# A linear-attention state in 32x32 tiles, output projections one head step earlier, and one row fetch moved ahead, in a fused attention and feed-forward kernel

## The reference

```python
# attn: 16 heads of 32 features; q, k, v, u = split(xn @ W_qkvu.T), q and k through silu
def step(kv, (qi, ki, vi)):                       # kv is [16, 32, 32]
    inter = (qi * q_decay) @ kv
    intra = ((qi @ ki.T) * diag_decay) @ vi
    kv = block_decay * kv + (ki * k_decay).T @ vi
    return kv, inter + intra
o = rms_normed(outs); attn = (u * o) @ W_out.T
# ffn: a router takes 256 of the 2048 rows; on them rms norm, q/k/v (16 heads of 128, 8 kv heads),
# rotary embedding, causal attention, wo, rms norm, silu(h @ w_gate) * (h @ w_up) @ w_down,
# gated with the router's sigmoid and put back at their places
```

## Time and profile before

| | |
|---|---|
| median of 3 runs | 508.22 us (507.51 to 508.35) |
| the profiled execution | 508.65 us |
| its span, first to last instruction | 506.9 us |
| granted clock of PE, mean | 0.990 |
| busy: PE, DVE, ACT, POOL | 486.5, 305.4, 231.6, 214.4 us |

### The profile page before, as it was taken

The page is one execution under the profiler, slowest core; times in us unless marked ns, Lnnn a source line. Parts: engine busy times, 40 slices in busy tenths (PEclk is TensorE's granted clock), DMA queues, the critical chain, the costliest instruction groups (busy, mean ns, idle before and its releaser), DMA issues.

```text
span 506.9 us, 10501 instructions
## 1 busy us (share of the span) xinstructions
PE 486.5 (96%) x4143; PEld 445.5 (88%) x4143; DVE 305.4 (60%) x615; ACT 231.6 (46%) x404; POOL 214.4 (42%) x191
## 2 busy tenths in 40 slices
PE   6998999999999999999999989799999999999994
PEld 6998899899998998999989888698888878999993
DVE  5879657764379888672555687997665535231221
ACT  7921132212255766512234226564667774545420
POOL 4002254232113311324268597434444413688872
PEclk8999999999999999999999999899999999999998
DMA  7924234113300110003525345354567462355503
GB/s 242 373 93 133 75 127 121 44 47 105 126 22 22 46 43 22 22 22 88 182 87 205 89 165 187 126 184 128 178 197 269 151 204 83 103 191 186 166 1 41
DMA packets 32880, 62.05 MB, mean 122 GB/s; under 512 B 3440, under 2 KB 3456, under 8 KB 32704
## 3 DMA queue, kind: packets, MB, share of 16 engines
q1 hardware_dynamic: 32288, 60.08, 36.0%
q0 software_dynamic: 544, 1.31, 1.4%
HBM read 48.27 MB, written 13.12 MB: 121 GB/s over the span
## 4 chain that ended last, share of the span: by engine, by line
PE 81%; DVE 8%; issue 3%; ACT 1%; POOL 0%; DVEq 0%; POOLq 0%
PE bank L1213 23%; PE bank L1167 10%; PE bank L1169 10%; PE bank L1168 10%; PE bank L1204 8%; PE bank L1276 3%; PE bank L1266 3%; PE bank L1232 3%; PE bank L1260 3%; DVE rope L862 3%; PE bank L1422 2%; PE bank L1443 1%; DVE rope L859 1%; DVE A L782 1%; PE bank L1183 1%
## 5 line engine op out<-in xcount | busy, mean ns | idle before, releaser
L1106 POOL TENSOR_TENSOR wlo<-raw,whi 128x512 fp32r<-128x512 f32 x96 | 125.5, 1341 | 86.7 <-ACT whi L516 86.7
L1091 POOL TENSOR_TENSOR state<-kv_new,state_dec 128x512 f32<-128x512 f32 x15 | 22.3, 1487 | 116.8 <-DVE kv_new L793 116.8
L1167 PE MATMUL bank<-HTh,whi 128*128 128x256 f32 x224 | 65.0, 290 | 3.0 <-DVE rope L862 3.0
L1169 PE MATMUL bank<-HTh,wlo 128*128 128x256 f32 x224 | 63.4, 283 | 0.0
L1168 PE MATMUL bank<-HTl,whi 128*128 128x256 f32 x224 | 63.3, 283 | 0.0
L782 DVE TENSOR_TENSOR A<-bank,DEC 128x512 f32<-128x512 f32 x64 | 39.7, 681 | 30.2 <-PE bank L1232 29.9
L516 ACT ACTIVATE whi<-raw 128x2048 fp32r<-128x2048 f32 x24 | 45.8, 1907 | 11.9 <-PE bank L1169 11.9
L1167 PEld LDWEIGHTS bank<-HTh,whi 128*128 128x128 f32 x224 | 42.9, 191 | 4.3 <-issue 3.8
L1168 PEld LDWEIGHTS bank<-HTl,whi 128*128 128x128 f32 x224 | 42.9, 192 | 0.3
L1169 PEld LDWEIGHTS bank<-HTh,wlo 128*128 128x128 f32 x224 | 42.9, 192 | 0.0
L1213 PE MATMUL bank<-xTh,WKh 128*128 128x256 f32 x128 | 37.5, 293 | 0.0
(11 more groups left out here) (237 smaller groups left out, 1361.3 us busy)
## 6 DMA issues: line engine op xcount, KB each, us to landing
X<-in_x SPq DMA_DIRECT2D x16, 256.0 KB, 4.5
xn_all<-XN SPq DMA_DIRECT2D x16, 256.0 KB, 2.7
uo_all<-uo SPq DMA_DIRECT2D x16, 256.0 KB, 2.4
raw<-in_wq SPq DMA_DIRECT2D x4, 1024.0 KB, 5.6
UR<-uo_all SPq DMA_DIRECT2D x16, 256.0 KB, 3.4
XR<-in_x SPq DMA_DIRECT2D x16, 256.0 KB, 3.1
raw<-in_wo SPq DMA_DIRECT2D x4, 1024.0 KB, 5.6
out<-XR SPq DMA_DIRECT2D x16, 256.0 KB, 2.1
```

Source lines behind the costliest of these rows:

```text
L1091: Q.tensor_tensor(state[:], kv_new[:], state_dec[:], ALU.add).then_inc(state_ok, 1)
L1106: ins = Q.tensor_tensor(low[:, k, :], raw[b % 3][:, k, :], high[:, k, :].bitcast(f32), ALU.subtract)
L1167: T.matmul(dst, lh, rh, start=first, stop=False)
L1169: return T.matmul(dst, ll, rh, start=False, stop=last)
```

## The change

The state, its decayed copy and the addition shrink to the 16 blocks of 32x32 (`[128, 4, 32]`). The carried-state product becomes 16 matmuls of 32 rows, 32 output rows and 128 columns, tile (r, r) for head 4j + r, all into `out_bank`; the new keys and values become 16 matmuls of 128 rows, 32 output rows and 32 columns. The mask and POOL's addition go; DVE adds straight from the bank. Output projections stand in steps 1 to 7 and 9 to 14, with the splits, the row fetches, the stores and the second fetches of x moved with them. SP fetches tile 4's rows ahead of the input and the stores of slot -1. PE turns tile 2 behind position 2.

```diff
-        qdec, sq, state, state_dec, kv_new = (at(n, kb, [P, NK, P]) for n, kb in (
-            ("qdec", 178), ("sq", 180), ("state", 184), ("state_dec", 186), ("kv_new", 188)))
+        qdec, sq = (at(n, kb, [P, NK, P]) for n, kb in (("qdec", 178), ("sq", 180)))
+        state, state_dec = (at(n, kb, [P, NK, DH]) for n, kb in (("state", 184), ("state_dec", 186)))
...
-        PT_AT, PV_AT, WO_AT, OUT_AT = 2, 3, 4, 2
+        PT_AT, PV_AT, WO_AT = 2, 3, 4
+        out_steps = [1, 2, 3, 4, 5, 6, 7, 9, 10, 11, 12, 13, 14]
+        out_at = {h: n for n, h in enumerate(out_steps)}
...
-            bank_jobs += [("out", h - OUT_AT)] if 0 <= h - OUT_AT < late_outs[0] else []
+            bank_jobs += [("out", out_at[h])] if h in out_at else []
...
             for N in slots_of_chunks:
+                if N == -1:
+                    load_xn(N + XT_AHEAD + 1)
                 for M in ln_tiles(N):
                     if M + 2 < N_TILES:
                         load_x(M + 2)
                     store_xn(M)
-                if NXN <= N + XT_AHEAD + 1 < N_TILES:
+                if NXN < N + XT_AHEAD + 1 < N_TILES:
                     load_xn(N + XT_AHEAD + 1)
...
             for h in range(STEPS):
-                if 2 <= h + 1 < N_TILES:
-                    load_uo(h + 1)
-                if 0 <= h - OUT_AT < late_outs[0]:
-                    store(h - OUT_AT)
-                if 2 <= h < N_TILES:
-                    load_x_again(h)
+                if h in out_at:
+                    n = out_at[h]
+                    load_uo(n + 2)
+                    store(n)
+                    load_x_again(n + 2)
+                    if h == out_steps[-1]:
+                        load_uo(n + 3), load_x_again(n + 3)
...
-                if 0 <= n + 1 < late_outs[2]:
-                    split_uo(n + 1)
+                if h == 0:
+                    split_uo(0)
+                if h in out_at:
+                    split_uo(out_at[h] + 1)
+                if h == out_steps[-1] + 1:
+                    split_uo(late_outs[1])
...
-            def state_part(N):
-
-                dve.wait_ge(kv_ps, N + 1), dve.wait_ge(state_ok, N)
-                V.tensor_tensor(kv_new[:], tiles4(turn_bank[:]), BM[:].unsqueeze(1).to_broadcast([P, NK, P]), ALU.mult)\
-                    .then_inc(kv_masked, 1)
+            def new_state(N):
+
+                dve.wait_ge(kv_ps, N + 1), dve.wait_ge(state_dk, N + 1)
+                V.tensor_tensor(state[:], turn_bank[:, 0:P].rearrange("p (k e) -> p k e", k=NK), state_dec[:], ALU.add)\
+                    .then_inc(state_ok, 1)
...
-                Q.tensor_tensor(state_dec[:], state[:], bdec.unsqueeze(2).to_broadcast([P, NK, P]), ALU.mult)\
+                Q.tensor_tensor(state_dec[:], state[:], bdec.unsqueeze(2).to_broadcast([P, NK, DH]), ALU.mult)\
                     .then_inc(state_dk, 1)
-
-            def new_state(N):
-
-                pool.wait_ge(kv_masked, N + 1), pool.wait_ge(state_dk, N + 1)
-                Q.tensor_tensor(state[:], kv_new[:], state_dec[:], ALU.add).then_inc(state_ok, 1)
...
-                for j in range(NK):
-                    ins = T.matmul(out_bank[:, j * P:(j + 1) * P], state[:, j, :], qdec[:, j, :], start=j == 0,
+                for h in range(NH):
+                    j, r = h // 4, h % 4
+                    rows = slice(DH * r, DH * r + DH)
+                    ins = T.matmul(out_bank[rows, j * P:(j + 1) * P], state[rows, j, :], qdec[rows, j, :], start=j == 0,
                                    stop=False, skip_group_check=True)
...
-                for j in range(NK):
-                    cols = slice(j * P, (j + 1) * P)
-                    ins = T.matmul(turn_bank[:, cols], kdec[:, cols], VT[N // CH % 2][:, N % CH, cols], start=True,
-                                   stop=True)
+                for h in range(NH):
+                    j, r = h // 4, h % 4
+                    cols = slice(DH * h, DH * h + DH)
+                    ins = T.matmul(turn_bank[DH * r:DH * r + DH, j * DH:(j + 1) * DH], kdec[:, cols],
+                                   VT[N // CH % 2][:, N % CH, cols], start=True, stop=True)
...
                 if N < 0:
                     in_position(N, 0)
                     in_position(N, 1)
-                    transposed(N + XT_AHEAD)
+                    if N == -1:
+                        transposed(N + XT_AHEAD)
                     in_position(N, 2)
+                    if N == -2:
+                        transposed(N + XT_AHEAD)
                     in_position(N, 3)
```

More of the change, by code:

```diff
@@ L270, in build @@
         q_dec, kt_ps, k_dec = sems("q_dec kt_ps k_dec")
-        s_ps, masked, inter_ps, kv_ps, kv_masked, pv_ps = sems("s_ps masked inter_ps kv_ps kv_masked pv_ps")
+        s_ps, masked, inter_ps, kv_ps, pv_ps = sems("s_ps masked inter_ps kv_ps pv_ps")
         state_dk, state_ok, uo_ok, sq_ok, sum_sq, rms_ps, ms_ok, r_ok = sems(
@@ L277, in build @@
         rank_ok, cnt_ps, oh_ok, idx_ps, idx_ok, pick_read = sems("rank_ok cnt_ps oh_ok idx_ps idx_ok pick_read")
-        dve_chain, pool_chain = sems("dve_chain pool_chain")
+        dve_chain, pool_chain, state_zero = sems("dve_chain pool_chain state_zero")
         fw_hi, fw_lo = sems("fw_hi fw_lo")
@@ L616, in _ @@
             for h in range(STEPS):
[L617 to L619 removed]
+                p, g = h - PT_AT, h - PV_AT
+                if h == 0:
[4 more added lines that the diff above has]
+                    split_uo(late_outs[1])
                 if h < FH:
@@ L636, in _ @@
                     normalised(h)
-                if 0 <= n < late_outs[0]:
-                    base(n)
+                if h in out_at:
+                    base(out_at[h])
                 if h in hi_after:
@@ L953, in _ @@
                 if 0 <= N < N_TILES - 1:
-                    state_part(N)
+                    new_state(N)
                 if N >= N_TILES - CH:
@@ L963, in _ @@
             for h in range(STEPS):
-                g, n = h - PV_AT, h - OUT_AT
+                g = h - PV_AT
                 if h < FH:
@@ L973, in _ @@
                     ins.then_inc(sm_ok, 1)
-                if 0 <= n + 1 < late_outs[2]:
-                    uo_low(n + 1)
+                if h == 0:
+                    uo_low(0)
+                if h in out_at:
+                    uo_low(out_at[h] + 1)
+                if h == out_steps[-1] + 1:
+                    uo_low(late_outs[1])
                 if h < FH:
@@ L982, in _ @@
                     stage(unit_of_step[h])
-                if 0 <= n < late_outs[0]:
-                    final(n)
+                if h in out_at:
+                    final(out_at[h])
                 if 0 <= g < FH:
@@ L1109, in _ @@
             ln_rstd(range(CH))
-            Q.memset(state[:], 0.0)
-            Q.memset(BM[:], 1.0).then_inc(pool_chain, 1)
-            blocks = BM[:].rearrange("p (r m) -> p r m", r=4)
-            pool.wait_ge(pool_chain, 5)
-            Q.affine_select(out=blocks, in_=blocks, compare_op=ALU.is_ge, fill=0.0, base=0, pattern=[[-DH, 4], [0, DH]],
-                            channel_multiplier=1).then_inc(pool_chain, 1)
-            pool.wait_ge(pool_chain, 6)
-            Q.affine_select(out=blocks, in_=blocks, compare_op=ALU.is_ge, fill=0.0, base=DH - 1,
-                            pattern=[[DH, 4], [0, DH]], channel_multiplier=-1).then_inc(bm_ok, 1)
+            Q.memset(state[:], 0.0).then_inc(state_zero, 1)
             ln_rstd(range(CH, NXN))
@@ L1249, in keys_turned @@
             def keys_turned(N):
-                pe.wait_ge(xt_lo, min(N + XT_AHEAD, N_TILES)), pe.wait_ge(kv_masked, N)
+                pe.wait_ge(xt_lo, min(N + XT_AHEAD, N_TILES)), pe.wait_ge(state_ok, N)
                 for k in range(NK):
@@ L1434, in _ @@
                     ins.then_inc(pt_ps, 1)
-                if 0 <= h - OUT_AT < late_outs[0]:
-                    project_out(h - OUT_AT)
+                if h in out_at:
+                    project_out(out_at[h])
                 g = h - PV_AT
```

11 lines of the change are left out of this document (4 added, 7 removed).

## The result

The median went from 508.29 us (4 runs, 507.51 to 509.08) to 502.78 us (4 runs, 501.76 to 504.35), a ratio of 0.9884 with a 95% interval of 0.9858 to 0.991. That is a gain of 5.5 us where 2.4 were forecast; the time lies in the range. The profiled execution took 502.39 us (span 500.7) against 508.65: 6.26 us less.

The account below looks back on a forecast made before the run. PE was taken to bound the kernel, busy 486.5 of 506.9 us. The sum was 508.65 - 2.4 + 0.55 - 0.55 + 0 = 506.25 us, 505.8 against the median, with a range of 502.0 to 511.0.

Parts of the forecast that it names:

- State products: PE's three state products per chunk: 2.94 us instead of 3.11, -0.17 a chunk in slots 0 to 13, -2.4 us.
- Removed from DVE and POOL: Mask product, POOL's wide addition, wider decay and mask set-up go: 0 us, because PE is saturated or nothing waits.
- Start: Third tile turned after Q's first projection: DVE's chain 1.1 us later, smaller decay gains about 0.55; net +0.55 us.
- Fifth tile's rows: Their fetch moved ahead of the stores on SP's queue: 0, since PE's turn waited for DVE's keys.
- Head steps: First head steps: output projection moved to step 1, one 2.9 us wait before unit 10, DVE not earlier; -0.55 us.
- Loads: Row fetches in head steps: issued 5.8 to 8.7 us before their split, 3.4 us landing stays hidden; 0.
- The gap at step 8: Head step 8 without an output projection: about 6 us long, in which DVE needs 5; 0.
- Clock: Low clock behind the gap before unit 10: costs 1.7 us before and stays, as the new gap is no shorter; 0.
- rival 3: Both ends close: slot 14's wait before the seventh unit shrinks by 0.7, low clock (1.7) does not come; 503.4 us, chance 0.13.
- rivals, 1: Narrow tiles keep wide ones' pace: third product 0.80 us, chunk +0.19, 510.9 us against the median; chance 0.14.
- Rival 2: Diagonal carried-state tiles do not overlap in one bank: 3.6 us instead of 0.98, +2.6 in 16 chunks, about 548 us; chance 0.07.
- Rival 4: PE's saving is given back to DVE's chain or to form changes: 508.2 us, chance 0.16.

Follow-up runs that it names:

- the run of the state part: Kernel before with only the edits to the state and its products (16 tiles for both products, DVE's addition, no mask): 502.59 us, ratio 0.9873.
- holding POOL back: Kernel before with the output projections moved, plus POOL's low part of step 0's weight block waiting for DVE's addition for unit 8: 512.09 us, ratio 1.0068.
- the order test: Kernel after with the 16 diagonal carried-state products issued row tile by row tile, so neighbours in the queue use the same tile: 523.12 us, ratio 1.0292.
- the head steps alone: Kernel before with only the output projections moved (steps 1 to 7 and 9 to 14, with their splits and DMAs): 513.1 us, ratio 1.0082.
- the start alone: Kernel before with only the third tile turned after Q's first projection and the fifth tile's rows fetched ahead: 510.13 us, ratio 1.0023.

## Why the prediction was right, and where its steps were not

The sign, the place and the time in the range were right; the forecast was 3.0 us above the median of after. That it came so close is partly luck: in the traces three terms gave 7.7 us more than forecast together (products 4.2, start 1.4, head steps 2.1), and the last steps, forecast at 0, took 3.75 back.

- **State products, forecast -2.4.** Right in mechanism, mis-sized. The term that failed is the third product: 0.44 + 0.20 was taken, 0.41 came in all, since its 32 records start within 0.28 us and the next form follows 0.13 behind the last. The carried-state product took 1.01, the lower bound, not the 1.09 of the score. With 0.08, 0.90 and 0.22 nearly as forecast, the chunk gained 0.49 where 0.17 was forecast, and 0.46 was the bound. Over the fourteen chunks that is 6.6 us by the starts.
- **Removed from DVE and POOL, forecast 0.** True for the chunks: POOL lost 30.7 us of work and nothing followed. In slots 14 and 15 the saving of PE was given back (-7.53, then -7.54), as forecast; the gap before the seventh unit grew from 1.31 to 1.80. False at the start. "POOL work before anything waits for it" failed: beside POOL's zeroing of the wide state and the mask's first row, DVE's first normalisation takes 0.87 instead of 0.55, and another 0.4 us of DVE's idle time went with this part.
- **Start, forecast +0.55.** The +1.1 for the reorder was the right mechanism and too small: 1.5 us where the state part is in. The relief from the smaller decay was right: 0.55 forecast, 0.64 measured (1.25 to 0.61). What the sum left out are the 0.3 and 0.4 us of the item above. In all, the traces with the state part start chunk 0 between 1.5 and 2.6 us earlier (47.49 to 47.67 against 49.16 to 50.05, tile turned first in both); these three make up to 1.4 us of it, and the rest is not assigned. Net -0.9 in this pair of traces.
- **Fifth tile's rows, forecast 0.** Right. No DMA is named before the turn, and with the tile turned first chunk 0 starts at 47.67 without this edit and at 47.49 to 47.56 with it.
- **Head steps, forecast -0.55.** Exact beside the kernel before (-0.51 in the run of this part alone), and -2.6 in the kernel after. The step that failed is "DVE cannot be earlier": DVE's addition came 0.07 us ahead of POOL's block instead of 0.02 behind it and took 0.69 instead of 1.80. Neither part alone brought this (1.73 in the run of the state part, 1.79 in that of the head steps), and holding POOL back did. Behind the gap of 1.75 that was left the clock did not fall.
- **Loads, forecast 0.** Failed, in both its numbers. "At 3.4 us to land it stays hidden" took the landing time of the old order; right behind a 1 MB block it is 5.6 us. And the rows were to leave one step, 5.8 to 8.7 us, before their split; in step 14 the queue comes to them 3.5 us into the step, behind a store at 396.30 and the block, 2.7 us before ACT wants them. Swapping the issues of rows and blocks brought 3.0 us.
- **The gap at step 8, forecast 0.** Not shown wrong: the run without it was faster, but with the rows ahead of their block in the same edit.
- **Clock, forecast 0.** The low clock behind the gap before unit 10 went, as rival 3 had it, and came back behind the new gap at 407. In sum 0, for another reason.

Of the rivals, 1 is refuted by the third product at 0.41. Rival 2 is refuted by the first product at 1.01, though the order test shows that the overlap it doubted is what the product lives on. Rival 3 came nearest in time (503.4), but half of its mechanism was absent: slot 14 gave nothing. Rival 4 happened, in slots 14 and 15 (0.5 a chunk) and in step 15, but took only a part.

The Trainium skill, "TensorE: Matmul & The Clock Gate", section "Back-to-back issue gap", gave 0.80 us for the third product by its 25 ns, an estimate that counted each of the 32 records as a matmul in one row. The trace has the 32 starts within 0.28 and does not agree for the four tiles together; on one tile the records start 28 to 32 ns apart, which stays above the page's figure. The Trainium skill, "PSUM — Partial Sum Buffer", section "PSUM bank collisions raise a hardware error", quotes that different row tiles cannot access one bank at the same time. The trace does not agree for tiles like these: the diagonal tiles, which write different partitions of one bank, start 32 records in 0.81 us here, where one after the other they are 0.11 apart.

The three parts alone sum to -6.1 + 4.4 + 1.45 = -0.2 us, the whole to -5.5. Part of the difference can be seen in the profiled executions: in the whole, the gap before unit 10 is 1.75 instead of the 2.94 of the head steps alone (1.2), and the clock was low for 3.4 us instead of 10.2 (half of the 6.8, 3.4). The executions of the state part and of the start alone each have a stretch of 3.41 at the low clock in the chunk slots, where that of before has none; it took 1.2 and 1.5 us. Besides, the state part's has the unexplained 1.7 us. The whole's has neither. So these two executions understate what their parts are worth. How much of the medians this explains is not shown.

## What to carry to other kernels

When an issue on a DMA queue is moved, look at what stands directly ahead of it, not at its median landing time: 256 KB behind 1 MB took 5.6 us instead of 3.7, and the consumer wanted them after 2.7. Price a narrow tiled product by the rounds of all its tiles together, and put consecutive products in the same form; splitting a full product into diagonal tiles gained nothing by itself here (1.01 us against 0.98). And where a part of a change is a loss alone, undo it in the full kernel too: here the start's order cost 1.2 us in the medians inside a change that gained 5.5.

## What the runs showed of the hardware that was not expected

- 32 records of 32 columns over four column tiles start within 0.28 us, 9 ns from one to the next on average: the four tiles 6 to 7 ns apart, one tile's next record 28 to 32 ns after its last.
- The same 16 diagonal products take 1.01 or 2.39 us by their order over the row tiles; neighbours on one tile start 0.11 apart.
- Two 128x512 operations of DVE and POOL that want to start at the same time: 0.69 us for DVE when it is 0.07 ahead, 1.80 when it is 0.02 behind. Holding POOL back gave the same 0.69.
- The clock fell to 1.2 GHz behind PE idling of 2.03 us (the start alone), 1.60 + 1.10 (step 15 after) and 2.52 to 3.09 (the first head steps, in five runs). The idle time alone does not decide: behind 1.62 + 1.10 in step 15 of the run row tile by row tile it stayed up, and behind the 1.80 of slot 15 it fell in two runs and not in six others. Two of these have the same program up to there, and the one with the low clock took 18.68 us from chunk 14 to chunk 15 instead of 17.19.
